# Causal score maxima on Trainium2: the mask added by TensorE, plain maxima on VectorE, and other groups in the weight fold

## The reference

```
x = LN(x + rwkv(x))                  # k, v, r = x @ W.T; weighted running sums; @ Wo.T
x = LN(x + ffn(x))                   # fwht(x*SU_ug); silu(x@W_gate.T * s1) * (x@W_up.T * s2);
                                     # fwht(.*SU_dp) / 64; @ W_down.T * (Wscale_dp*64)
x = LN(x + attention(x))             # 16 heads of 32; q and k times sin|cos; causal softmax(q k / sqrt(32)) v
x = LN(x + moe(x))                   # top 2 of 8 experts, and a shared one
```

## Time and profile before

| | |
|---|---|
| median of 3 runs | 1499.97 us (1498.73 to 1501.67) |
| the profiled execution, its own time | 1497.31 us |
| its span, first to last instruction | 1495.6 us |
| TensorE | 7681 matmuls, 97% of the span |
| VectorE | 1841 instructions, 62% |
| ScalarE | 1007 instructions, 41% |
| GpSimd | 455 instructions, 36% |

### The profile page before, as it was taken

One profiled execution on the slowest core, in us unless ns is written; L12 is line 12 of the kernel. 1 busy time (PEld: TensorE's weight loads), 2 busy tenths in 40 slices (PEclk: granted clock), 3 DMA queues, 4 the chain that ended last, 5 costly groups with the idle time before them and its releaser, 6 DMA issues. The chain is left out here.

```text
span 1495.6 us, 22377 instructions
## 1 busy us (share of the span) xinstructions
PE 1448.1 (97%) x7681; PEld 1077.8 (72%) x7696; DVE 928.9 (62%) x1841; ACT 609.5 (41%) x1007; POOL 545.7 (36%) x455
## 2 busy tenths in 40 slices
PE   7999989999999999999999999999999999999887
PEld 5788768788888888888888785555555457777554
DVE  6887887855544554554243475766666468667664
ACT  5343455622431341243121114555556636442544
POOL 0333243302430441143152223444444576104773
PEclk9999999999999999999999998999999999999999
DMA  6111447503330431131445888677775464844337
GB/s 211 43 58 57 173 152 250 198 28 102 113 95 0 158 95 55 45 124 58 176 145 178 243 236 226 185 198 191 199 194 150 163 223 167 324 175 139 102 103 242
DMA packets 105226, 223.37 MB, mean 149 GB/s; under 512 B 9328, under 2 KB 35312, under 8 KB 104240
## 3 DMA queue, kind: packets, MB, share of 16 engines
q1 hardware_dynamic: 101392, 211.96, 44.3%
q0 software_dynamic: 3744, 10.23, 2.2%
HBM read 157.54 MB, written 64.36 MB: 148 GB/s over the span
## 5 line engine op out<-in xcount | busy, mean ns | idle before, releaser
L969 POOL TENSOR_TENSOR ff_w_lo<-ff_raw,ff_w_hi 128x1024 fp32r<-128x1024 f32 x64 | 153.5, 2399 | 219.6 <-ACT ff_w_hi L999 205.4
L115 PE MATMUL op_bank<-ff_x_hi,ff_w_lo 128*128 128x512 f32 x512 | 199.4, 390 | 0.0
L117 PE MATMUL op_bank<-ff_x_hi,ff_w_hi 128*128 128x512 f32 x512 | 199.4, 389 | 0.0
L116 PE MATMUL op_bank<-ff_x_lo,ff_w_hi 128*128 128x512 f32 x512 | 199.4, 389 | 0.0
L1239 DVE TENSOR_TENSOR ff_h_lo<-ff_hf,ff_h_hi 128x512 f32 (+1 forms) x64 | 146.3, 2286 | 53.7 <-ACT ff_h_hi L1127 53.4
L2075 ACT ACTIVATE at_pt<-at_st 128x512 f32<-128x512 f32 (+1 forms) x286 | 145.0, 581 | 71.5 <-PE at_st L2118 69.9
L1384 DVE CUSTOM_DVE_ANT_0 mx_mx<-mx_mx,mx_mask 128x128 f32<-128x128 f32 (+2 forms) x200 | 101.5, 517 | 40.6 <-PE mx_mx L1372 39.4
L999 ACT ACTIVATE ff_w_hi<-ff_raw 128x1024 fp32r<-128x1024 f32 x64 | 67.8, 1061 | 118.4 <-PE op_bank L117 115.9
L115 PEld LDWEIGHTS op_bank<-ff_x_hi,ff_w_lo 128*128 128x128 f32 x512 | 96.1, 188 | 20.2
L116 PEld LDWEIGHTS op_bank<-ff_x_lo,ff_w_hi 128*128 128x128 f32 x512 | 96.2, 188 | 20.0
L117 PEld LDWEIGHTS op_bank<-ff_x_hi,ff_w_hi 128*128 128x128 f32 x512 | 96.2, 188 | 19.9
(11 more groups left out here) (478 smaller groups left out, 3441.0 us busy)
## 6 DMA issues: line engine op xcount, KB each, us to landing
ff_raw<-in_Wug SPq DMA_DIRECT2D x64, 512.0 KB, 3.7
at_raw<-in_expert_gu SPq DMA_DIRECT2D x16, 704.0 KB, 7.7
mx_qp<-q_hi SPq DMA_DIRECT2D x12, 512.0 KB, 6.5
mx_kp<-k_hi SPq DMA_DIRECT2D x12, 512.0 KB, 10.9
at_raw<-in_expert_d SPq DMA_DIRECT2D x8, 768.0 KB, 9.6
expert_gu_bf<-at_cast SPq DMA_DIRECT2D x16, 352.0 KB, 5.7
ex_e_gu<-expert_gu_bf SPq DMA_DIRECT2D x8, 704.0 KB, 8.3
tm_ln_res<-in_x SPq DMA_DIRECT2D x4, 1024.0 KB, 5.4
```

The source lines that it names most:

```text
L115: pe.matmul(out, cut_l(ll), cut_r(rh), start=first, stop=False, **kw)
L116: pe.matmul(out, cut_l(lh), cut_r(rl), start=False, stop=False, **kw)
L117: return pe.matmul(out, cut_l(lh), cut_r(rh), start=False, stop=last, **kw)
L969: pool.tensor_tensor(w[j][1][:, :, :, :], raw[:, j], f32(w[j][0][:, :, :, :]), ALU.subtract)\
```

## The change

The mask becomes 128 x 128, and GpSimd casts it and the identity to bf16. TensorE cuts a diagonal piece in two: the keys ahead of the last 128, and the last 128. To the latter it adds identity times mask with a third matmul. VectorE takes a plain maximum of every piece. VectorE's waits for the mask are gone; TensorE and GpSimd have them. The fold's groups become 2, 2, 3, 3, 3 and 3 tiles, and the stores end at tiles 4, 10, 13 and 16 where they ended at 6, 12, 15 and 16.

```diff
-    GROUP, RING = 3, 5
-    GROUPS = -(-NCH // GROUP)
-    STORED = [6, 12, 15, NCH]
+    GROUPS, RING = (2, 2, 3, 3, 3, 3), 5
+    STORED = [4, 10, 13, NCH]
     STORE_AFTER = [5, 7, 9, 9]
...
-        return range(g * self.GROUP, min((g + 1) * self.GROUP, NCH)) if g >= 0 else range(0)
+        return range(sum(self.GROUPS[:g]), sum(self.GROUPS[:g + 1])) if g >= 0 else range(0)
...
-        self.ident, self.mask = b.sb("ident", [P, P]), b.sb("mask", [P, TB])
+        self.ident, self.mask = b.sb("ident", [P, P]), b.sb("mask", [P, 3 * P])
+        self.ident_b, self.mask_b = b.sb("ident_b", [P, P], BF16), b.sb("mask_b", [P, P], BF16)
...
-        sp.dma_start(self.mask[:, TB - P:], a["causal"]).then_inc(self.small_loaded, DMA)
+        sp.dma_start(self.mask[:, 0:P], a["causal"]).then_inc(self.small_loaded, DMA)
...
     def open_mask(self, pool):
-        pool.memset(self.mask[:, 0:TB - P], 0.0).then_inc(self.open_set, 1)
-        pool.wait_ge(self.open_set, 1)
+        pool.wait_ge(self.small_loaded, 2 * DMA)
+        pool.tensor_copy(self.ident_b[:, :], self.ident[:, :]).then_inc(self.open_set, 1)
+        pool.tensor_copy(self.mask_b[:, :], self.mask[:, 0:P]).then_inc(self.open_set, 1)
...
-        pe.matmul(bank[:, 0:hi - lo], self.qp[j][0:R_MAX, h, qt * P:(qt + 1) * P],
-                  self.kp[j][0:R_MAX, h, lo:hi], start=True, stop=True).then_inc(self.piece_done, 1)
+        rows = self.qp[j][0:R_MAX, h, qt * P:(qt + 1) * P]
+        own = qt * P if hi == (qt + 1) * P else hi
+        if own > lo:
+            mm = pe.matmul(bank[:, 0:own - lo], rows, self.kp[j][0:R_MAX, h, lo:own], start=True, stop=True)
+        if own < hi:
+            pe.matmul(bank[:, own - lo:hi - lo], rows, self.kp[j][0:R_MAX, h, own:hi], start=True, stop=False)
+            mm = pe.matmul(bank[:, own - lo:hi - lo], self.ident_b[:, :], self.mask_b[:, :], start=False, stop=True)
+        mm.then_inc(self.piece_done, 1)
...
-        if hi == (qt + 1) * P:
-            dve.tensor_tensor_reduce(piece, piece, self.mask[:, TB - (hi - lo):], 1.0, -3e38, ALU.add, ALU.max, out)\
-                .then_inc(self.piece_read, 1)
-        else:
-            dve.reduce_max(out, piece, AX.X).then_inc(self.piece_read, 1)
+        dve.reduce_max(out, piece, AX.X).then_inc(self.piece_read, 1)
...
                 if pieces and pieces[0] == 0:
                     pe.wait_ge(mx.small_loaded, 2 * DMA)
+                    pe.wait_ge(mx.open_set, 2)
...
-                    if of == 0:
-                        dve.wait_ge(mx.small_loaded, 2 * DMA)
-                        dve.wait_ge(mx.open_set, 1)
```

## The result

The changed kernel takes 1516.57 us (1513.14 to 1517.05, 3 runs) where the kernel before took 1499.97: a ratio of 1.0112 (1.0097 to 1.0126), that is 14.5 to 18.9 us more. Forecast were 12.8 more, 1512.8, in a range of 1498 to 1524.

What follows compares the result with a forecast made beforehand. TensorE, busy in 97% of the span, was taken as the bound. Opening 4.4, attention 10.1 and fold -1.7 sum to +12.8 us: 1510.1 for the profiled execution, 1512.8 as a median, range 1498 to 1524.

Steps and rivals of the forecast that it cites:

- The price of a matmul: On TensorE, a matmul costs its columns (512: 0.23 us), at least 0.12 before fp32 weights; 128 columns before bf16 weights, 0.06.
- Opening: First 48 score pieces, among the projections: added matmuls paid in full, 3.9 us, plus 0.5 for low clock, +4.4.
- Attention: Bursts of score matmuls and pieces: waiting for VectorE covers part of the added matmuls, the rest costs +10.1 us.
- Fold: Groups of two remove TensorE's two waits for a third tile, some waiting returns in step 3: -1.7 us.
- Loads and conversions: GpSimd waits for identity and mask, some 3.5 us late, but TensorE's path is not delayed: 0 us.
- Rival 1: Bursts: VectorE sets the pace, a 128-wide matmul costs 0.06 whatever its weights; faster, 1494.4 us, chance 0.14.
- Rival 2: No change: bursts cover everything, the opening pays 4.4, the fold gives its whole 4.0; 1500.4 us, chance 0.10.
- Rival 3: Attention: pieces reach VectorE later, so TensorE waits as long as now, behind more work; 1531.5 us, chance 0.06.
- Rival 4: Fold: no gain, tiles wait elsewhere as long; 1514.5 us, within the forecast's range, no chance of its own.
- The signs: Traces: also bursts of 3.24, 3.13, 3.26 us growing 0.15 to 0.4, those of 3.98 and 4.30 staying.
- store chain: Fold: the last store waits for tile 15 and holds up bring-back and weight chunk, limiting the gain to -1.7 us.
- signs of being wrong: Shorter bursts, VectorE waits as long as now, new fold waits beyond 2 us, or changed stretches at 1.2 GHz.

Runs made afterwards that it cites:

- mask_only: The changed kernel with the old fold groups and stores, so only cut, mask matmul and plain maxima are new: 1517.13 us, ratio 1.012 to the kernel before.
- fold_only: The kernel before with only the new fold groups and stores, maxima as before: 1496.24 us, ratio 0.9977; run again, 1496.69 us, 0.999.
- plain_max: The kernel before with a plain maximum of every piece, the mask left out of the maxima: 1496.51 us, ratio 0.9976.
- mask_first: Against mask_only, the mask's matmul stands ahead of that of the last 128 keys: 1523.43 us, ratio 1.0147 to the kernel before.
- mask_uncut: Against mask_only, a diagonal piece stays one matmul, with the mask added onto its last 128 columns: 1512.89 us, ratio 1.0087 to the kernel before.
- cut_only: Against mask_only, pieces are cut but no mask is added, and it is left out of the maxima: 1501.55 us, ratio 1.0009 to the kernel before.

## Why the prediction was right, step by step

**The price of a matmul** was the base, and it held. In the projections, where TensorE is full, the 48 pieces cost:

| change to the pieces | by the price | measured |
|---|---|---|
| cut and mask | 3.9 | 4.0 (changed kernel), 4.0 (mask_only, against fold_only) |
| mask without the cut | 8 x 0.42 = 3.4 | 3.3 (47.12 against fold_only's 43.83) |
| cut without the mask | 2.0 | 1.5 |
| mask ahead of the last 128 | 1.4 more | 1.2 more |
| mask in 4 bytes | 1.6 to 1.9 more | 1.1 more |

The Trainium skill, "TensorE: Matmul & The Clock Gate", section "LDWEIGHTS (loading the stationary operand)", gives the time of a load in ns as its columns over 1.2, an estimated 107 ns for 128; the 0.11 us between the fp32 loads of the earlier trace rows agrees. In these runs the format counts as well: the matmul behind the mask starts 0.04 us after it where the mask is bf16, and 0.11 where it is 4 bytes wide.

**Opening, +4.4**: measured 4.02. The 0.5 for a low clock at the first four pieces did not show: with a stretch at half clock in both (before, changed) or in neither (mask_only, fold_only) the difference is 4.0.

**Attention, +10.1**: measured 11.8, or 12.2 from the end of the pieces in the projections. The first unit was put at 3.7 and took 3.6; its first burst, at half clock, grew by 2.8 where 2.9 were forecast. The full units were put at 1.1 and took 1.4. The uncovered parts of the first four bursts, 0.21, 0.40, 0.15 and 0.21, were 0.38, 0.33, 0.13 and 0.25. What was mis-sized is the cover of the last two: their spare 0.89 and 0.61 was to swallow all, and left 0.17 and 0.18. Against plain_max, which has VectorE's gain alone, a unit pays 1.7 of 4.0 (38.51 to 40.22): 2.3 are covered, and 0.9 of waiting stays. I read this so that a wait covers only the matmuls added ahead of it in its burst; that was not tried apart. VectorE's own part was put at 0.1 more in a unit, its gain and the delay by the mask together; plain_max shows the gain alone, 0.3 less.

**Fold, -1.7**: fold_only gives -3.8 and, in its second round, -2.0. The size came out about right and its parts did not, so that is luck. Of the 3.5 us of old waits 1.7 were to come back in step 3; 2.2 came there, and 0.5 more in step 5, so that waiting alone gave less than 1 us. The restart of weight loads was put at 0.5 for both old waits; in the changed kernel the matmul behind a wait takes 0.34 to the next start (218.32 to 218.66) where 0.23 is its price, 0.1 a wait. The store chain did take back SyncE's lead, from 2.4 to 0.6, as forecast, but TensorE did not lose by it: it leads by 1.46 at step 8 and by 1.41 at step 12. What made up for the waits was not in the sum. Between the kernel before and the changed one, 1.18 of the 1.46 us are there at the first step already, ahead of the new order, behind the stretch at half clock that only the kernel before has at 188.65. Between mask_only and fold_only it is 2.4 us to step 8 (76.04 and 73.64): 1.2 are waiting (3.9 and 2.7), and the stretch of 3.41 us at half clock that is gone, worth an estimated half of it, 1.7, is more than enough for the other 1.2. I had named the clock as what could upset the forecast, and priced it at nothing.

**Loads and conversions, 0**: right. GpSimd waited for the mask as forecast, and TensorE did not. GpSimd's timeline of the changed kernel there:

```profile
759.41 0.56 POOL L1360 CAST mx_ident_b<-mx_ident 128x128 bf16<-128x128 f32 x1 [5.02 <-DMA mx_mask<-in_causal]
759.93 0.29 POOL L1361 CAST mx_mask_b<-mx_mask 128x128 bf16<-128x128 f32 x1
760.18 2.53 POOL L1568 TENSOR_TENSOR qkv_part_lo<-qkv_whole,qkv_part_hi 128x512 fp32r<-128x512 f32 x2
```

**The rivals.** Rival 1 (extra matmuls stream) fell: no burst is shorter, and mask_first shows that order sets the price. Rival 2 fell with the bursts. Rival 3 (nothing is covered) fell: waits for VectorE shrank from 3.1 to 0.9 a unit, to less than the third that was named; its price takes 6.2 for the first unit, where the forecast's own 2.9 and 2.4 make 5.3. Rival 4 (the fold doesn't gain) is nearly right in its reason, for most of the waiting came back elsewhere, and fell in its time: fold_only's first round is clear of no change, though its second is not, and to step 8 it is 2.4 us ahead of mask_only.

**The signs.** Four signs of being right came: 448 more matmuls, waits down to a third, the longer opening, the two old waits gone. Of the bursts, the two that were to stay grew by 0.17 and 0.18, and the third grew by 0.13 where at least 0.15 was named. Two signs of being wrong came as well. The fold has new waits of 2.8 us, over the 2 that were named. And the stretches at 1.2 GHz changed: the one at 188.65 is gone, attention's went from 13.65 to 17.07, and one of 3.41 came in the expert layer. In sum, without the one that ends each trace, they went from 20.5 to 23.9 us, worth an estimated half of the 3.4, 1.7 us. So the forecast of the maxima part came out by its mechanism, and that of the fold did not.

In the profile, the stages touched sum to 4.02 + 0.39 + 11.78 - 1.46 = 14.7, at the lower end of the measured 14.5 to 18.9. The forecast's 12.8 is 1.9 under that, mostly by the 0.3 in each of the five full units. The other 1.9 us up to the measured 16.6 are put down to no stage here.

## What to carry to other kernels

Before moving work from an engine at 62% to one at 97%, price the added instructions on the busy one by a neighbour's delay, not by their own starts: the mask looked like 0.04 us and cost 0.13. Check in each stretch which idle time stands behind the added work, and count only that as cover. And when a mask serves only to bound a maximum that cancels later, try leaving it out first: on these inputs that was faster than both ways of adding it.

## What the runs showed of the hardware

TensorE's granted clock fell to 0.50, that is 1.2 GHz, around the end of attention's first wait, 3.1 us for GpSimd in the kernel before and in the changed one. The stretch lasts 13.65 us in the kernel before, and 17.07 in all four kernels with cut and mask; the windows of before and of the changed kernel:

```profile
905.45:919.10 13.65, 13.65 (x49) 9.44 (x51) 9.38 (x29) 6.10 (x11) 5.68 (x5) 0.50 0.93 300
908.25:925.32 17.07, 16.95 (x74) 12.74 (x77) 9.03 (x17) 6.15 (x11) 6.12 (x6) 0.50 0.92 271
```

In mask_uncut it is 13.65, and there the first unit grew by 1.9 where it grew by 3.6 in the changed kernel and by 3.4 in mask_only. In cut_only, which has added matmuls too, it is 10.24. So cut and mask together were followed by a longer time at 1.2 GHz, and in the one profile of either alone they were not; why is not shown. The fold shows the other side: a wait that was split and shortened saved about as much by the clock (at most 1.7, half of 3.41) as by the waiting itself (3.9 in mask_only against 2.7 in fold_only).
